# Attention with a quantising stream on VectorE: where the stream's steps and the projection jobs are placed

## The chip, the cores and the metric

One Trainium2 chip. The same program runs on all eight cores, each with one batch row of 2048 tokens. The metric is the device time of the slowest core in microseconds, the median of the runs.

## The reference

One transformer layer whose attention and feed-forward part both read the same normalised tokens:

```python
xn = _layernorm(x)                        # x: (8, 2048, 1024), one batch row a core
# attention, 16 heads of 64
q, k, v = xn @ wq.T + bq, xn @ wk.T + bk, xn @ wv.T + bv
scores = einsum(q, k) * 64 ** -0.5;  masked where x[..., 0] == 0
attn = softmax(scores) @ v;  a = attn @ wo.T + bo
# feed-forward with quantised operands, hidden size 4096
h = bit_linear(xn, w1)                    # tokens rounded to 127 steps of their largest value,
h = silu(depthwise_conv1d(h))             # weights to -1, 0, 1 by the mean of their absolute values
f = bit_linear(h, w2)
out = x + a + f
```

So the weights w1 and w2 have to be read once for the mean of their absolute values and once more to be rounded, and each token row has to be scaled and rounded, before the feed-forward part can start.

## The kernel before

Attention comes first, the feed-forward part second. This text concerns attention. Its main loop has 512 **steps**, one for each pair of a query block and a key tile: 8 head pairs times 4 query blocks of 512 are 32 iterations (`NIT`) of 16 key tiles (`NT`) each. Every engine has its program written out step by step by Python loops.

- **ACT** (`a_scalar`) takes one exponential of 128x1024 at a step (L363).
- **PE** (`a_tensor`) does at step *i*: `scores(i+1)` (L445, two matmuls into one of two halves of psS), then the **pieces** that the planner put on this step (`piece`, L386), then `pv` (L462, eight small matmuls) for the steps of `pv_at`. The values of steps 0, 1 and 2 of an iteration are put off by 2, 1 and 1 steps, to give the norm time.
- A piece is one matmul of a **job**. Jobs are: `k`, `q` and `v` (projections of head pairs or value columns, eight matmuls each, L397, L406, L413), `t` (transpose of the finished context, L419), `x` (transpose of half a quantised token tile, L425, two halves a tile) and `m` (the sum for the means of the weights, L429). Jobs take two PSUM slots in turn (`slot`): the first piece of a job waits on `pq_ev` until DVE has evicted the job two before it. An `x` piece also waits for the token tile (`xq_w`), a `t` piece for the norm (`cn_w`).
- **DVE** (`a_vector`) runs strictly in order. At step *i*: at position 1 of an iteration the `norm` of the iteration before (L594, L599: reciprocal and product, which first waits for the last values of it, and which the first values of the new iteration wait for), then the **stream** of this step (`strm_task`), then `evac` of the jobs whose last piece stood at this step (k L552, q L560 and L562, v L565 and L568, t L573, x L576).
- The stream has 64 weight chunks `w` (one sum of absolute values of 128x1024 each, L610), 16 token tiles `x` in four parts (scale L616; largest value L620; four small ones L623 to L628; round L631 and L638), `m` (L644, L645), a gap, and 64 chunks `z` in three parts (quantise a weight chunk, L652, L655, L663).
- **SP** (`a_sync`) loads the chunks and tiles of the stream into four buffers in turn; the load of item n waits until item n-4 is done.
- **POOL** (`a_gload`) loads projection weights of the next head pairs when k and q jobs are done with a buffer (L309, L311), and later the output weights.

**Two planners** in `_build` set the order. The first (L153 to L177) places the stream: five chunks to a token tile, every part at a share of the steps that goes by a table of weights, over the steps 3 to 487 other than positions 0 and 1 of an iteration. The second (L179 to L224) places the jobs: each has a due step; at each step a credit (`cap_full`, `cap_less`) says how many pieces may be taken; small jobs (t, x, m) go first; and a job may begin only some steps (`evac_steps`) after the job two before it ended. Token transposes are due two steps after the last part of their tile:

```python
for n, step in ready_x.items():
    due[("x", n, 0)] = due[("x", n, 1)] = step + 2
due[("m", 0, 0)] = ready_m + 2
```

Of the kernel before, what the change touches and what calls it, by code (L numbers as in the profile page):

```python
# [16 lines left out]
NT = T // 128  # L17
# [17 lines left out]
def _build():  # L35
# [103 lines left out]
    NW = W1CH + W2CH  # L139
    NIT = NHP * NQB  # L140
    NSTEP = NIT * NT
# [11 lines left out]

    strm_items = []
    for n in range(NT):
        strm_items += [("w", ch) for ch in range(5 * n, min(5 * n + 5, NW))]
        if 5 * n < NW <= 5 * n + 5:
            strm_items.append(("m", 0))
        strm_items.append(("x", n))
    strm_items += [("gap", 0)] + [("z", ch) for ch in range(NW)]  # L160
    weight = {"w": 2.5, "x": 4.6, "m": 1.0, "gap": 8.0, "z": 3.7}
    parts = {"w": 1, "x": 4, "m": 1, "gap": 0, "z": 3}
    total_w = sum(weight[k] for k, _ in strm_items)
    free_steps = [i for i in range(3, NSTEP - 24) if i % NT not in (0, 1)]
    step_strm = {i: [] for i in range(NSTEP)}
    ready_x, ready_m = {}, 0
    acc = 0.0
    for kind, n in strm_items:
        for part in range(parts[kind]):
            pos = acc + weight[kind] * part / parts[kind]  # L170
            i = free_steps[int(pos / total_w * len(free_steps))]
            step_strm[i].append((kind, n, part))
            if kind == "x" and part == 3:
                ready_x[n] = i
            if kind == "m" and part == 0:
                ready_m = i
        acc += weight[kind]  # L177

    step_pieces = {i: [] for i in range(NSTEP)}  # L179
    n_pieces = {"k": 8, "q": 8, "v": 8, "t": 1, "x": 1, "m": 1}  # L180
    piece_cost = {"k": 1.0, "q": 1.0, "v": 0.55, "t": 0.3, "x": 0.3, "m": 0.5}
    evac_steps = {"k": 2, "q": 3, "v": 2, "t": 2, "x": 2, "m": 2}
    cap_full = [1.2, 2.4, 2.4, 0.6, 0.6] + [1.8] * 11
    cap_less = [1.0, 2.0, 2.0, 0.4, 0.4] + [1.2] * 11
    due = {}
    for it in range(NIT):
        hp, s0 = it // NQB, it * NT
        big = [("v", (2 * it + m) % NT, 1 + (2 * it + m) // NT) for m in range(2)
               if 2 * it + m < 3 * NT]
        if hp < NHP - 1:  # L190
            big.insert(0, ("k", hp + 1, it % NQB))
        if it < NIT - 2:
            big.append(("q", it + 2, 0))
        for m, job in enumerate(big):
            due[job] = s0 + (0, 4, 8, 10)[m]
        if it >= 1:
            due[("t", it - 1, 0)] = s0 + 5
    for n, step in ready_x.items():
        due[("x", n, 0)] = due[("x", n, 1)] = step + 2
    due[("m", 0, 0)] = ready_m + 2  # L200
    wait_list = sorted(due, key=lambda jb: due[jb])
    ends = [-9, -9]
    kinds = ["v", "v"]
    cur, nxt = None, 0
    credit = 0.0
    for step in range(NSTEP):
        cap = cap_full if step < 25 * NT else cap_less
        credit = min(credit + cap[step % NT], 4.0)
        while credit > 0.3:
            if cur is None:  # L210
                ready = [jb for jb in wait_list if due[jb] <= step]
                if not ready or step < ends[-2] + evac_steps[kinds[-2]]:
                    break
                small = [jb for jb in ready if jb[0] in "txm"]
                cur, nxt = (small or ready)[0], 0
                wait_list.remove(cur)
            step_pieces[step].append((cur, nxt))
            credit -= piece_cost[cur[0]]
            nxt += 1
            if nxt == n_pieces[cur[0]]:  # L220
                ends.append(step)
                kinds.append(cur[0])
                cur = None
    assert cur is None and not wait_list, (cur, wait_list)  # L224
    first_z = min(i for i in range(NSTEP) for e in step_strm[i] if e[0] == "z")
    done_at = {jb: step for step in range(NSTEP) for jb, p in step_pieces[step]}
    assert done_at[("m", 0, 0)] < first_z and done_at[("x", NT - 1, 1)] < first_z
    assert all(done_at[("q", it, 0)] < it * NT - 2 for it in range(2, NIT))
    assert all(done_at[("k", hp, b)] < hp * 64 + 4 * b - 2 for hp in range(1, NHP) for b in range(4))
    assert all(done_at[("v", ti, q)] < q * 128 + ti - 1 for q in range(1, 4) for ti in range(NT))  # L230
    last_piece = {k: n - 1 for k, n in n_pieces.items()}
    step_jobs = {i: [j for j, p in step_pieces[i] if p == last_piece[j[0]]] for i in range(NSTEP)}
    for i in range(NSTEP):
        jobs += step_jobs[i]
# [1027 lines left out]
```

## Time and profile before

| | us |
|---|---|
| median of 3 runs (lowest, highest) | 1194.06 (1193.83, 1195.04) |
| profiled execution, its own time | 1195.17 |
| its span, slowest core (all cores 1190.2 to 1193.6) | 1193.6 |
| attention's loop, first to last exponential, in the profile | 90.4 to 650.0 |
| mean granted TensorE clock, cores | 0.984 to 0.987 |

How it is read: a row of a group gives the line, engine, tiles and shapes, the count, the busy time in us and the mean of one in ns, then the idle time of the engine before it and who ended it. A line of a timeline gives start and length in us; consecutive instructions of one line stand together with their count, and since matmuls overlap, their lengths are longer than their spacing. All rows below are of the slowest core, core 7.

### The profile page before, as it was taken

Reading aid. Unit: us, or ns where it says so; the run is one execution under the profiler, and the core shown is the slowest. Engines: PE = TensorE matmul, PEld = TensorE weight load, DVE = VectorE, ACT = ScalarE, POOL = GpSimd, SP = SyncE. Lnnn points to the kernel's source line nnn. Section 1 sums busy time; section 2 is a strip of 40 time slices with the busy share of each in tenths; the row PEclk is TensorE's granted clock in tenths of the full one; section 3 lists DMA queues with packets and bytes.
Section 4 is the critical chain, followed back from the end, with each engine's and each line's share of the span. In section 5 each row is a group of like instructions: output and inputs, shape, how many; then the busy total and the mean of one; then the engine's idle time right before and its main releaser. Section 6 shows DMA issues by size and latency. Waiting matters only on the chain.

```text
span 1193.6 us, 28386 instructions; the slowest of 8 cores (1190.2 to 1193.6 us)
## 1 busy us (share of the span) xinstructions
PE 1090.4 (91%) x9138; PEld 591.9 (50%) x9138; DVE 891.8 (75%) x1519; ACT 815.8 (68%) x1115; POOL 222.6 (19%) x177
## 2 busy tenths in 40 slices
PE   1579999999989999999988999989999999999698
PEld 0345555566555666555555444444444444444243
DVE  4646787888887888887872788877777777777676
ACT  2559888888878999999998444566666666555100
POOL 1000000000000000000022133233323333434374
PEclk9789999999999999999999999989999999999999
DMA  8636756546543676856584456564454454553252
GB/s 216 183 44 163 184 162 173 174 150 192 164 125 81 167 181 164 192 155 180 160 194 129 152 166 182 165 193 116 144 157 137 146 149 143 150 151 116 71 170 95
DMA packets 84717, 183.06 MB, mean 153 GB/s; under 512 B 25184, under 2 KB 29664, under 8 KB 84576
## 3 DMA queue, kind: packets, MB, share of 16 engines
q1 hardware_dynamic: 79248, 172.52, 49.4%
q0 software_dynamic: 4032, 8.39, 4.9%
q8 instruction: 80, 1.31, 0.5%
q14 instruction: 61, 0.50, 0.1%
q10 hardware_dynamic: 1296, 0.34, 0.1%
HBM read 164.44 MB, written 25.17 MB: 159 GB/s over the span
## 4 chain that ended last, share of the span: by engine, by line
PE 73%; ACT 12%; DVE 7%; issue 5%; DMA 1%; DVEq 0%; ACTq 0%; POOL 0%; SPq 0%; POOLq 0%
PE psC L869 17%; PE psA L887 16%; PE psS L445 13%; ACT probs L363 11%; PE psV L462 7%; PE psA L855 5%; PE psQ L397 5%; PE psQ L413 4%; PE psQ L406 3%; PE psC L887 2%; DMA xhead<-x 1%; DVE hq L1061 1%; PE psX L879 1%; PE psX L887 1%; PE psS L381 0%
## 5 line engine op out<-in xcount | busy, mean ns | idle before, releaser
L363 ACT ACTIVATE probs<-psS 128x1024 bf16<-128x1024 f32 x512 | 504.0, 1022 | 55.6 <-PE psS L445 42.3
L445 PE MATMUL psS<-qz,kroll 128*128 128x512 bf16 x1024 | 304.5, 378 | 16.7 <-ACT probs L363 12.0
L869 PE MATMUL psC<-xqT,w1q_sb 128*128 128x512 bf16 x1024 | 242.9, 381 | 0.0
L887 PE MATMUL psA<-w2q_sb,hq 128*128 128x512 fp8e4 x896 | 216.0, 382 | 16.7 <-DVE hq L1061 16.7
L462 PEld LDWEIGHTS psV<-v_sb,probs 128*128 128x128 bf16 x4096 | 183.0, 97 | 76.4 <-issue 2.1
L780 POOL TENSOR_TENSOR h_act<-h_act,shb_sb 128x512 f32<-128x512 f32 x128 | 164.3, 1286 | 251.3 <-DVE hq L1061 198.2
L462 PE MATMUL psV<-v_sb,probs 128*128 128x65 bf16 x4096 | 198.4, 193 | 0.7 <-ACT probs L363 0.5
L869 PEld LDWEIGHTS psC<-xqT,w1q_sb 128*128 128x128 fp8e4 x1024 | 99.3, 98 | 116.6 <-issue 1.9
L887 PEld LDWEIGHTS psA<-w2q_sb,hq 128*128 128x128 bf16 x896 | 87.5, 98 | 126.5 <-issue 25.2
L1010 DVE SCALAR_TENSOR_TENSOR u_sb<-psC,cws,u_sb 128x511 f32<-128x511 f32 x128 | 95.8, 749 | 71.4 <-ACT u_sb L805 71.2
L805 ACT ACTIVATE u_sb<-psC,cws 128x510 f32<-128x510 f32 (+2 forms) x128 | 87.5, 683 | 57.6 <-PE psX L879 56.1
L799 ACT ACTIVATE u_sb<-psC,edge,cws 128x1 f32<-128x1 f32 x96 | 33.8, 352 | 125.3 <-PE psC L869 125.3
L1013 DVE SCALAR_TENSOR_TENSOR u_sb<-psC,cws,u_sb 128x511 f32<-128x511 f32 x128 | 96.0, 750 | 13.7 <-DVE u_sb L1010 0.5
L1061 DVE TENSOR_SCALAR hq<-h_act,meff,meffneg 128x512 bf16<-128x512 f32 x128 | 92.5, 725 | 17.0 <-PE psX L887 9.4
L815 ACT ACTIVATE h_act<-u_sb,cbc 128x512 f32<-128x512 f32 x128 | 92.2, 720 | 0.0
L445 PEld LDWEIGHTS psS<-qz,kroll 128*128 128x128 bf16 x1024 | 67.8, 98 | 47.3 <-issue 39.4
L413 PE MATMUL psQ<-wv_sb,xnT 128*128 128x256 bf16 x512 | 77.8, 276 | 3.1 <-ACT xnT L349 1.9
L397 PE MATMUL psQ<-xnT,wqk 128*128 128x512 bf16 x256 | 78.9, 399 | 1.8 <-DVE xqT L576 1.7
L824 ACT ACTIVATE ab<-h_act 128x512 f32<-128x512 f32 x128 | 80.1, 626 | 0.1
L406 PE MATMUL psQ<-xnT,wqk 128*128 128x512 bf16 x256 | 79.1, 380 | 0.2 <-DVE xqT L576 0.2
L309 POOL DMA_DIRECT2D wqk<-wk_t x6 | 3.2, 529 | 399.9 <-PE psQ L406 399.9
L610 DVE TENSOR_REDUCE wsum<-strm 128x1 f32<-128x1024 f32 x64 | 76.9, 1211 | 0.2
(104 smaller groups left out, 1035.0 us busy)
## 6 DMA issues: line engine op xcount, KB each, us to landing
strm<-w_t SPq DMA_DIRECT2D x128, 512.0 KB, 4.3
w2q_sb<-w2q_stage SPq DMA_DIRECT2D x112, 256.0 KB, 2.6
w1q_sb<-w1q_stage SPq DMA_DIRECT2D x64, 256.0 KB, 2.9
xhead<-x SPq DMA_DIRECT2D x16, 512.0 KB, 5.6
strm<-x SPq DMA_DIRECT2D x16, 512.0 KB, 4.9
xarea<-x SPq DMA_DIRECT2D x16, 512.0 KB, 6.3
res_stage<-xarea SPq DMA_DIRECT2D x16, 512.0 KB, 3.6
xarea<-res_stage SPq DMA_DIRECT2D x16, 512.0 KB, 6.5
```

Source lines behind the costliest of these rows:

```text
L363: s.activation(out=probs[:, (i % NP) * 1024:(i % NP + 1) * 1024], in_=psS[:, (i % 2) * 1024:(i % 2 + 1) * 1024], func=AF.Exp, scale=0.125, ...
L397: mm = t.matmul(ps, wqk[:, o:o + 128], xnTv[:, p, b * 512:(b + 1) * 512], start=(p == 0), stop=(p == 7))
L406: mm = t.matmul(ps, wqk[:, o:o + 128], xnTv[:, p, qb * 512:(qb + 1) * 512], start=(p == 0), stop=(p == 7))
L413: mm = t.matmul(ps[:, 0:256], xnTv[:, p, a * 128:(a + 1) * 128], wv_sb[:, b * 2048 + p * 256:b * 2048 + (p + 1) * 256], start=(p == 0), st ...
L445: mm = t.matmul(psS[:, (g % 2) * 1024 + hh * 512:(g % 2) * 1024 + (hh + 1) * 512], kTv[:, hp % 2, kc * 128:(kc + 1) * 128], qz[:, (it % 4) ...
L462: mm = t.matmul(psV[:, hh * 512 + qt * 65:hh * 512 + (qt + 1) * 65], probs[:, o:o + 128], v_v[:, kc, 2 * hp + hh, :], start=(kc == 0 and q ...
L780: g.tensor_tensor(h_unit(r), h_unit(r), shb_unit(r), OP.mult).then_inc(sem("f_qa"), 1)
L869: mm = t.matmul(mbank(g), w1q_sb[:, o + cc * 256:o + cc * 256 + 128], xqTv[:, cc, tb * 512:tb * 512 + 512], start=(cc == 0), stop=(cc == N ...
L887: return t.matmul(gbank(k, j), hq[:, o:o + 128], w2q_sb[:, w:w + 512], start=(jc == 0), stop=(jc == NJC - 1))
L1010: v.scalar_tensor_tensor(ua[:, 1:512], ps[:, 0:511], cws[:, jc * 3:jc * 3 + 1], ua[:, 1:512], OP.mult, OP.add).then_inc(sem("f_o2"), 1)
L1013: tap3 = v.scalar_tensor_tensor(ua[:, 0:511], ps[:, 1:512], cws[:, jc * 3 + 2:jc * 3 + 3], ua[:, 0:511], OP.mult, OP.add)
L1061: v.tensor_scalar(hq_unit(r), h_unit(r), meff[:, 0:1], meffneg[:, 0:1], OP.add, OP.add).then_inc(sem("f_q"), 1)
```

## The change

The stream's plan no longer leaves positions 0 and 1 of an iteration free. The jobs are planned twice with one function, `place_jobs`. The first plan has no token and mean jobs; from it, each step gets a **room**: 1.1 us less what evictions (`evac_us`) and the norm (`norm_us`) take. The stream's parts (`part_us`) are then laid at steps so that they use the summed room in proportion. There are four chunks to a token tile in place of five, and the mean's sums stand before the last tile. Then the token jobs get due steps four (before: two) after their last part, the mean job too, and the jobs are planned again. The gap is 5.0 of the new units (before 8.0 of the old). What each engine executes is the same; the order in which it stands changes.

```diff
     for n in range(NT):
-        strm_items += [("w", ch) for ch in range(5 * n, min(5 * n + 5, NW))]
-        if 5 * n < NW <= 5 * n + 5:
-            strm_items.append(("m", 0))
-        strm_items.append(("x", n))
+        strm_items += [("w", ch) for ch in range(4 * n, 4 * n + 4)] + [("x", n)]
+    strm_items.insert(strm_items.index(("x", NT - 1)), ("m", 0))
     strm_items += [("gap", 0)] + [("z", ch) for ch in range(NW)]
-    weight = {"w": 2.5, "x": 4.6, "m": 1.0, "gap": 8.0, "z": 3.7}
-    parts = {"w": 1, "x": 4, "m": 1, "gap": 0, "z": 3}
-    total_w = sum(weight[k] for k, _ in strm_items)
-    free_steps = [i for i in range(3, NSTEP - 24) if i % NT not in (0, 1)]
...
+    part_us = {"w": [1.2], "x": [0.9, 1.2, 0.9, 1.8], "m": [0.3], "gap": [5.0],
+               "z": [0.8, 0.8, 0.9]}
+    evac_us = {"k": 0.75, "q": 1.55, "v": 0.6, "t": 0.75, "x": 0.65, "m": 1.0}
+    norm_us = 1.5
...
+    def place_jobs():
+        pieces = {i: [] for i in range(NSTEP)}
+        wait_list = sorted(due, key=lambda jb: due[jb])
+        ends, kinds = [-9, -9], ["v", "v"]
+        cur, nxt, credit = None, 0, 0
...
+        return pieces
+
+    step_pieces = place_jobs()
+    room = []
+    for i in range(NSTEP):
+        used = sum(evac_us[j[0]] for j, p in step_pieces[i] if p == last_piece[j[0]])
+        used += norm_us if i % NT == 1 and i >= NT else 0
+        room.append(1.1 - used)
+    room_at, acc = [], 0.0
+    for i in range(NSTEP):
+        acc = max(0.0, acc + room[i]) if 3 <= i < NSTEP - 24 else acc
+        room_at.append(max(acc, room_at[-1] if i else 0.0))
+    total_us = sum(sum(part_us[k]) for k, _ in strm_items)
...
+    for kind, n in strm_items:
+        for part, us in enumerate(part_us[kind]):
+            pos = acc / total_us * room_at[-1]
+            i = next(i for i in range(NSTEP) if room_at[i] > pos)
+            if kind != "gap":
+                step_strm[i].append((kind, n, part))
...
+            acc += us
     for n, step in ready_x.items():
-        due[("x", n, 0)] = due[("x", n, 1)] = step + 2
-    due[("m", 0, 0)] = ready_m + 2
...
+        due[("x", n, 0)] = due[("x", n, 1)] = step + 4
+    due[("m", 0, 0)] = ready_m + 4
+    step_pieces = place_jobs()
```

The body of `place_jobs` is the old planner's loop, unchanged.

## Rows read from the trace of the kernel before

**Rows 1.** The page, busy time of each engine over the span.
```profile
PE 1090.4 (91%) x9138; PEld 591.9 (50%) x9138; DVE 891.8 (75%) x1519; ACT 815.8 (68%) x1115; POOL 222.6 (19%) x177
```

**Rows 2.** Stretches: length, busy PE, PEld, DVE, ACT, POOL; clock, DMA share, GB/s.
```profile
619.20:650.00 30.80, 26.15 (x331) 15.68 (x327) 7.67 (x16) 30.66 (x32) 6.99 (x3) 1.00 0.67 178
...
124.50:216.80 92.30, 85.28 (x1014) 52.64 (x1013) 75.89 (x130) 79.14 (x81) 2.12 (x4) 1.00 0.61 168
216.80:234.60 17.80, 17.42 (x211) 10.79 (x209) 15.01 (x27) 15.84 (x17) 0.00 (x0) 1.00 0.46 154
234.60:342.60 108.00, 104.11 (x1223) 65.03 (x1220) 89.50 (x160) 95.19 (x97) 1.05 (x2) 1.00 0.56 168
342.60:366.10 23.50, 18.13 (x217) 10.92 (x214) 21.43 (x46) 15.63 (x17) 1.05 (x2) 1.00 0.36 91
366.10:384.00 17.90, 17.20 (x206) 11.12 (x207) 12.15 (x25) 15.99 (x17) 0.00 (x0) 1.00 0.29 71
384.00:521.70 137.70, 135.68 (x1585) 84.16 (x1584) 112.15 (x200) 126.93 (x129) 2.11 (x4) 1.00 0.72 175
486.80:521.70 34.90, 34.03 (x396) 21.14 (x394) 27.80 (x50) 31.54 (x33) 0.00 (x0) 1.00 0.75 182
```

**Rows 3.** Waits between 124.5 and 216.8 us: total, times, longest.
```profile
DVE rden L594 <- PE psV L462: 4.6, 3, 2.0
...
PE psQ L425 <- DVE kroll L552: 5.1, 5, 1.2
```

**Rows 4.** Timeline of PE around a token transpose.
```profile
205.84 0.59 PE L445 MATMUL psS<-qz,kroll 128*128 128x512 bf16 x2
206.27 0.59 PE L397 MATMUL psQ<-xnT,wqk 128*128 128x512 bf16 x2
206.70 0.41 PE L462 MATMUL psV<-v_sb,probs 128*128 128x65 bf16 x8
206.94 0.60 PE L445 MATMUL psS<-qz,kroll 128*128 128x512 bf16 x2
...
207.59 0.39 PE L419 MATMUL psQ<-identb_s,cn 128*128 128x128 bf16 x4
207.82 0.41 PE L462 MATMUL psV<-v_sb,probs 128*128 128x65 bf16 x8
...
208.86 0.59 PE L445 MATMUL psS<-qz,kroll 128*128 128x512 bf16 x2
210.54 0.38 PE L425 MATMUL psQ<-identb_s,qbuf 128*128 128x128 bf16 x4 [1.08 <-DVE kroll L552]
211.20 0.38 PE L425 MATMUL psQ<-identb_s,qbuf 128*128 128x128 bf16 x4 [0.28 <-DVE ctx L573]
```

**Rows 5.** Timeline of DVE in the same stretch.
```profile
203.45 1.22 DVE L610 TENSOR_REDUCE wsum<-strm 128x1 f32<-128x1024 f32 x1
204.59 0.81 DVE L616 TENSOR_SCALAR strm<-strm,negm,rstd 128x1024 f32<-128x1024 f32 x1
...
208.66 0.81 DVE L638 TENSOR_SCALAR qbuf<-strm,meffneg,tiny 128x1024 bf16<-128x1024 f32 x1 [0.18 <-DVE strm L631]
209.53 0.75 DVE L552 TENSOR_SCALAR kroll<-psQ,bkc 128x512 bf16<-128x512 f32 x1
210.20 0.74 DVE L573 TENSOR_SCALAR ctx<-psQ,bvc 128x512 bf16<-128x512 f32 x1
```

**Rows 6.** Waits between 342.6 and 366.1 us.
```profile
ACT probs L363 <- PE psS L445: 7.6, 6, 2.3
```

**Rows 7.** Groups of instructions over the span: evictions and the norm.
```profile
L599 DVE TENSOR_TENSOR cn<-psV,rden 128x256 bf16<-128x256 f32 x64 | 24.3, 420 | 1.2
...
L560 DVE TENSOR_SCALAR qz<-psQ,bqc 64x512 bf16<-64x512 f32 x32 | 23.7, 741 | 27.7 <-PE psQ L406 27.5
...
L576 DVE CAST xqT<-psQ 128x512 bf16<-128x512 f32 x32 | 21.4, 683 | 0.7 <-PE psQ L425 0.7
```

**Rows 8.** DMA issues of the page: count, size, us to landing.
```profile
strm<-w_t SPq DMA_DIRECT2D x128, 512.0 KB, 4.3
```

More of the change, by code:

```diff
@@ L155, in _build @@
     for n in range(NT):
-        strm_items += [("w", ch) for ch in range(5 * n, min(5 * n + 5, NW))]
-        if 5 * n < NW <= 5 * n + 5:
-            strm_items.append(("m", 0))
-        strm_items.append(("x", n))
+        strm_items += [("w", ch) for ch in range(4 * n, 4 * n + 4)] + [("x", n)]
+    strm_items.insert(strm_items.index(("x", NT - 1)), ("m", 0))
     strm_items += [("gap", 0)] + [("z", ch) for ch in range(NW)]
-    weight = {"w": 2.5, "x": 4.6, "m": 1.0, "gap": 8.0, "z": 3.7}
-    parts = {"w": 1, "x": 4, "m": 1, "gap": 0, "z": 3}
-    total_w = sum(weight[k] for k, _ in strm_items)
-    free_steps = [i for i in range(3, NSTEP - 24) if i % NT not in (0, 1)]
[L165 to L179, printed above, removed]
+    part_us = {"w": [1.2], "x": [0.9, 1.2, 0.9, 1.8], "m": [0.3], "gap": [5.0],
+               "z": [0.8, 0.8, 0.9]}
+    evac_us = {"k": 0.75, "q": 1.55, "v": 0.6, "t": 0.75, "x": 0.65, "m": 1.0}
+    norm_us = 1.5
     n_pieces = {"k": 8, "q": 8, "v": 8, "t": 1, "x": 1, "m": 1}
+    last_piece = {k: n - 1 for k, n in n_pieces.items()}
     piece_cost = {"k": 1.0, "q": 1.0, "v": 0.55, "t": 0.3, "x": 0.3, "m": 0.5}
@@ L197, in _build @@
             due[("t", it - 1, 0)] = s0 + 5
-    for n, step in ready_x.items():
-        due[("x", n, 0)] = due[("x", n, 1)] = step + 2
-    due[("m", 0, 0)] = ready_m + 2
[L201 to L223, printed above, removed]
@@ L224, in _build @@
-    assert cur is None and not wait_list, (cur, wait_list)
+    def place_jobs():
[3 more added lines that the diff above has]
+        cur, nxt, credit = None, 0, 0
+        for step in range(NSTEP):
+            cap = cap_full if step < 25 * NT else cap_less
+            credit = min(credit + cap[step % NT], 4.0)
+            while credit > 0.3:
+                if cur is None:
+                    ready = [jb for jb in wait_list if due[jb] <= step]
+                    if not ready or step < ends[-2] + evac_steps[kinds[-2]]:
+                        break
+                    small = [jb for jb in ready if jb[0] in "txm"]
+                    cur, nxt = (small or ready)[0], 0
+                    wait_list.remove(cur)
+                pieces[step].append((cur, nxt))
+                credit -= piece_cost[cur[0]]
+                nxt += 1
+                if nxt == n_pieces[cur[0]]:
+                    ends.append(step)
+                    kinds.append(cur[0])
+                    cur = None
+        assert cur is None and not wait_list, (cur, wait_list)
+        return pieces
@@ new lines, in _build @@
+    step_strm = {i: [] for i in range(NSTEP)}
+    ready_x, ready_m = {}, 0
+    acc = 0.0
+    for kind, n in strm_items:
[4 more added lines that the diff above has]
+                step_strm[i].append((kind, n, part))
+            if kind == "x" and part == 3:
+                ready_x[n] = i
+            if kind == "m":
+                ready_m = i
+            acc += us
@@ L230, in _build @@
     assert all(done_at[("v", ti, q)] < q * 128 + ti - 1 for q in range(1, 4) for ti in range(NT))
-    last_piece = {k: n - 1 for k, n in n_pieces.items()}
     step_jobs = {i: [j for j, p in step_pieces[i] if p == last_piece[j[0]]] for i in range(NSTEP)}
```

## The prediction

> **What bounds the kernel now.** I began with the busy table of the page [rows 1]: PE is the fullest engine (91%), DVE the second (75%); but that is an average over two halves, so the second view is the table of stretches. The change touches attention alone, 512 steps of one exponential each. I cut that part at the start of every 16th exponential, so a stretch holds whole query blocks of 16 steps (*blocks* 0 to 31; the ACT count is 16 for each block and one that straddles). The reader is to see four things in [rows 2]. Blocks 2 to 6 last 18.46 us each, block 7 17.8, blocks 8 to 13 18.0 each. Block 14 lasts 23.5, and there DVE is busy 21.43 us and PE only 18.13. Blocks 16 to 23, where no token tile is quantised, last 17.2 each with PE at 98%. The last two, which hold hardly any projection piece, last 15.4, so 0.96 us is the shortest step that ACT allows. PE's granted clock is 1.00 (2.4 GHz) in all these stretches, through the waits too.
>
> The third view, the waits of blocks 2 to 6, says who is late: PE waits at a token transpose for DVE's eviction of a k job, 5 times in 5 blocks, 5.1 us together [rows 3]. The timeline around one of them shows why. PE finished its scores at about 209.3 (208.86 and 0.43 for the pair, the spacing 205.84 to 206.27) and begins the first transpose at 210.54, the second at 211.20, where such a group has spacing 0.23 (207.59 to 207.82) [rows 4]. DVE ran the last part of the token's chain up to 209.47 and evicted k from 209.53 and ctx from 210.20, behind it [rows 5]; each transposed half needs the PSUM slot of the job two before it. So PE stood 1.24 + 0.43 = 1.7 us in this block. In block 14 the last three token tiles fall on 16 steps with no weight chunk left between them: the same wait comes several times, and ACT waits 7.6 us for scores [rows 6].
>
> **How I priced the change.** No instruction is added or removed: 64 chunk sums, 16 token chains, 64 chunks of quantising, the evictions and norms stay; only the step at which each stands moves. I wrote out the planner's rules of both versions into tables of what PE and DVE get at each step, and priced them. A PE step is 0.43 us of scores, 0.21 for a k or q piece (the pair from 206.27 to 206.70), half of that for a v piece of half the columns, 0.23 for a transposed half, 0.24 for values (206.70 to 206.94) [rows 4], never under 0.96 in all. DVE runs in order, an eviction after PE's last piece; a job's first piece waits for the eviction of the job two before. DVE's prices: chunk sum 1.14 from start to start (203.45 to 204.59), k or ctx 0.67 (209.53 to 210.20) [rows 5], q 1.5 for two halves of 0.74, token half 0.68, norm two multiplies of 0.42 and two short reciprocals, about 1.0 [rows 7]. One choice is left, spacings or durations: the chunk sum lasts 1.22 where the next instruction starts 1.14 after it, so neighbours overlap by 0.08 us [rows 5].
> The Trainium skill says otherwise (VectorE: DVE Perf Modes, The DRAIN you can't avoid): the next Vector instruction does not start until the pipeline of the one before has emptied. By that rule durations would be the price everywhere; the trace does not agree.
> With durations the new table is 4.9 us shorter than the old one, with spacings 6.7. Both misjudge stretches of the old kernel (durations give 25.4 us for block 14, the row 23.5), so I take the terms stretch by stretch and check them against the rows.
>
> *Block 14.* Before: three tiles. After: four chunks, one tile and the mean job, since with four chunks to a tile the sixteen tiles go evenly over steps 3 to 240, one in 15 steps. DVE's largest backlog, at 1.1 us a step, falls from 9.1 us (step 237) to 2.8 (step 33). The new tables give 17.4 and 18.1 us; I take 18.1, near the 18.0 of its neighbours: 18.1 - 23.5 = **-5.4 us**. Blocks 1 and 15: -0.3 and +0.3, nothing together.
>
> *Blocks 2 to 7.* The old wait goes: transposes are due 4 steps after the chain in place of 2, and the chain is done. What is late next is an eviction. The new plan puts a tile's two halves at steps 0 and 2 of each block, the k job right behind the second, q's last piece on step 15 and a chunk sum on step 0. From q's last piece: 0.17 until its result shows (the pair of [rows 4] lasts 0.59, its spacings 0.43), q 1.5, chunk 1.14, the first half 0.68: 3.5 us. PE comes to k after values 0.24, steps 0 and 1 at 0.96, scores 0.43 and a half 0.23: 2.8. It waits 0.7 there, each block; behind the waiting k piece stand the next scores, and ACT for them. The new plan is also lumpier: steps with no piece beside one of seven v and one of four k; an empty step costs ACT's 0.96 where PE has 0.67 of work. Both tables give +0.1 for each of blocks 2 to 6 (durations 18.45 for the old ones, the row 18.46) and +1.6 for block 7, which had no long wait before: **+2.2**.
>
> *Blocks 8 to 13.* The old plan waits in most of them (0.2 to 1.3 us by the tables); the new one in 8 and 9 (0.5 to 0.8, v behind k) and in 13 for the norm (0.6). Tables: -2.8 and -3.1; taken **-2.9**.
>
> *Blocks 16 to 23.* No long wait in either. But the job grid shifts: from block 16 on the new plan has in each block the layout that the old one reaches only in 22 and 23 (four k, three, one, none, four v ...). Those two last 17.45 each, all eight 137.7 [rows 2]: 8 x 17.45 - 137.7 = **+1.9**. Blocks 24 to 31 keep their pieces: 0.
>
> *Queues.* SP issues the same 80 loads into four buffers, each landing 4.3 us after its issue [rows 8]. The tightest run of the new plan uses four chunks in some six steps, over 5.5 us, so they stay hidden; if not, each late one costs DVE at most its landing. POOL's weight loads wait for k and q jobs that move by a few steps and are needed blocks later: nothing. The second half of the kernel is not touched.
>
> Sum: -5.4 + 2.2 - 2.9 + 1.9 = **-4.2 us**. The profiled execution took 1195.17 (span 1193.6), 1.1 over the median 1194.06; against it the sum gives 1191.0, against the median **1189.9 us**. A measurement of this kernel tells about 0.2% (2.4 us) from no change.
>
> **Rivals.**
> *The waits go altogether* (0.12). If PE never waits for a slot, blocks 2 to 13 fall to the 17.2 of those without token tiles: 218.1 - 12 x 17.2 = 11.7 less, 5.4 in block 14, 1.9 given back: 1179. For it: PE was busy 85.28 of 92.3 us in blocks 2 to 6. Against it: the arithmetic of step 2 has 0.7 us to lose.
>
> *The gain is handed back, the change does not do what it says* (0.20). DVE's room is measured on a first plan without token and mean jobs; the second plan puts 56 of the 79 evictions of the first half on another step, by up to 4. If the waits come out 0.3 us a block longer than priced in blocks 1 to 14, 4.2 is back: 1194.
>
> *DVE late at the turn of the block: slower* (0.13). The old plan keeps its stream off steps 0 and 1; the new one puts a chunk on step 0, in front of the norm of step 1, and in blocks 3, 5 and 7 one at step 15. Values of step 3 wait for the norm, k at step 2 for the eviction; by my prices the norm ends 0.6 us before it is needed. If DVE gets there 1.0 us later (a chunk ahead of q's eviction), both waits grow by it; in two thirds of 14 blocks that is +9.3: 1199. It decides from 0.3 us a block. For it: in blocks 2 to 6 DVE comes early to the norm in only 3 of 5 already [rows 3]. Against: a chunk of step 15 can run before q's last piece is there.
>
> **How the numbers follow.** The forecast case has 0.55 and its own range 1184 to 1192: with DVE 5% dearer the tables give 8 to 10 us less than before, with DVE 5% cheaper 1 to 3 (the old waits were smaller then). The larger gain has 0.12, none 0.20, slower 0.13. Range 1181 to 1197.5: it leaves out most of the largest gain and over half of the slow case, 0.18. Faster by over 0.2%: 0.12 and 0.53 of the forecast case, 0.65; within: 0.20 + 0.02 = 0.22; slower 0.13.
>
> **What would show it.** Block 14 near 18 us with DVE under 19 busy. In blocks 2 to 7 PE waits for the eviction of a token half at a k matmul, once a block, 0.7 to 1.1 long, in place of the transposes' wait for k. Blocks 16 to 23 near 139.6. The second half the same within 1 us. Wrong if block 14's time reappears in 13 or 15, if values wait for the norm in many blocks, or if the layout of blocks 16 to 23 costs nothing.

## The result, and the profile after

The changed kernel takes 1195.64 us (median of 20 runs) where the kernel before takes 1194.12: the ratio is 1.0014, with a 95% interval of 1.0007 to 1.002. It is slower by 0.14%, within the 0.2% that I called no change, though the interval leaves out 1. The forecast was 4.2 us faster. Three of the forty executions, two before and one after, were in a slower state (1308 to 1361 us); the ratio leaves them out.

In the changed kernel every line of the attention part stands 14 further down (scores L459, values L476, norm L608 and L613, chunk sum L624, eviction of a token half L590, quantising L666, L669, L677). The table of stretches of the changed kernel, cut at its own 16th exponentials: length, busy PE, PEld, DVE, ACT, POOL, clock, DMA share, GB/s.

```profile
123.60:216.90 93.30, 85.74 (x1022) 54.10 (x1021) 75.48 (x132) 79.54 (x80) 2.13 (x4) 1.00 0.57 161
216.90:236.20 19.30, 17.58 (x213) 11.16 (x212) 17.20 (x30) 15.76 (x16) 0.00 (x0) 1.00 0.55 178
236.20:342.10 105.90, 103.85 (x1235) 65.58 (x1233) 91.19 (x161) 94.85 (x97) 2.11 (x4) 1.00 0.54 166
342.10:359.70 17.60, 17.41 (x209) 11.21 (x206) 14.97 (x29) 15.87 (x17) 0.00 (x0) 1.00 0.68 180
359.70:377.30 17.60, 17.23 (x208) 10.89 (x204) 11.35 (x28) 15.83 (x18) 0.00 (x0) 1.00 0.23 55
377.30:516.90 139.60, 136.04 (x1571) 84.40 (x1569) 109.62 (x195) 126.28 (x128) 2.11 (x4) 1.00 0.66 162
...
614.60:635.30 20.70, 15.53 (x167) 9.16 (x164) 8.17 (x14) 15.51 (x16) 0.00 (x0) 0.84 0.78 202
620.00:625.00 5.00, 3.84 (x39) 2.67 (x40) 2.88 (x8) 1.02 (x1) 0.00 (x0) 0.50 1.04 267
650.70:1193.40 542.70, 517.63 (x2620) 239.20 (x2620) 411.67 (x617) 274.93 (x549) 196.95 (x141) 0.99 0.45 143
```

Set beside [rows 2]:

| blocks | before | forecast | after |
|---|---|---|---|
| 2 to 7 | 110.1 | +2.2 | 112.6 (+2.5) |
| 8 to 13 | 108.0 | -2.9 | 105.9 (-2.1) |
| 14 | 23.5 | -5.4 | 17.6 (-5.9) |
| 15 | 17.9 | +0.3 | 17.6 (-0.3) |
| 16 to 23 | 137.7 | +1.9 | 139.6 (+1.9) |
| 24 to 29 | 97.5 | 0 | 97.7 (+0.2) |
| 30 and 31 | 30.8 | 0 | 36.1 (+5.3) |

Up to block 30 the forecast nearly came true: its first exponential starts at 614.6 us where it started at 619.2. Of these 4.6 us 0.8 was there before the loop began (first exponential at 89.6 us, before 90.4), in code that the change does not touch. From there to block 30 the changed kernel takes 525.0 us where the old one takes 528.8, 3.8 less. Then block 30, one of those that keep their pieces, lasts 20.7 us where 15.4 was usual. The second half takes 542.7 us, 0.9 less than the 543.6 before; that is no more than the profiles of one kernel and another differ by in this stretch (541.7 to 544.4 over all of them). The loop as a whole lasts 561.1 us in place of 559.6, the 1.5 us by which the medians differ; the spans of these two executions (1193.4 and 1193.6) hide it. The loss is in that one block. Its chain of waits and its timelines show how (start, length, and in brackets the idle time before and who ended it). DVE:

```profile
614.63 0.76 DVE L666 TENSOR_SCALAR strm<-strm,sw 128x1024 f32<-128x1024 f32 x1 [1.41 <-DMA strm<-w_t]
...
619.64 0.75 DVE L666 TENSOR_SCALAR strm<-strm,sw 128x1024 f32<-128x1024 f32 x1 [2.08 <-DMA strm<-w_t]
620.31 0.24 DVE L608 RECIPROCAL rden<-psV 128x4 f32<-128x4 f32 x2
620.59 0.76 DVE L613 TENSOR_TENSOR cn<-psV,rden 128x256 bf16<-128x256 f32 x2
```

PE in the same stretch:

```profile
617.67 0.59 PE L459 MATMUL psS<-qz,kroll 128*128 128x512 bf16 x2 [0.41 <-ACT probs L377]
621.16 1.15 PE L476 MATMUL psV<-v_sb,probs 128*128 128x65 bf16 x16 [2.90 <-DVE cn L613]
622.12 1.04 PE L459 MATMUL psS<-qz,kroll 128*128 128x512 bf16 x2
```

The longest piece of the chain of waits there:

```profile
608.39 11.08 DMA strm<-w_t
```

The quantising part on step 480 (position 0 of block 30) waits for a chunk whose load took 11.1 us from 608.39 on, where 4.3 is the median [rows 8]. Behind it in DVE's order stands the norm of step 481; for the norm wait the values that stand on step 483 of PE, 2.90 us; behind them on PE stand the next scores, and for these ACT waits (3.88 us). PE's scores at 617.67 still have their full-clock length. After them PE stands from 618.26 on; the clock over 614.6 to 620 us is 0.95, so it falls only shortly before 620, and from 620 to 625 it is half (1.2 GHz): the two score matmuls at 622.12 last 1.04 us in place of 0.59.

What holds the load back are the output-weight loads. POOL issues eight of them, of 256 KB each, from 602.8 to 607.5 us, once the last k, q or v job (step 466) is done. The DMA engines are full (a share over 1 says that the times of the packets add up to more than the stretch of the 16 engines). The issues, and the ten microseconds before the wait ends:

```profile
L776 POOL DMA_DIRECT2D wo_bf<-wo_t x8: 527/661/1015, 602.8 to 607.5; - x8
...
610.00:620.00 10.00, 6.70 (x66) 3.30 (x65) 5.56 (x8) 9.37 (x10) 0.00 (x0) 0.97 1.07 228
```

The old kernel has the same contention, and its DVE waited for loads as well. There the same chunk belongs to step 479. DVE could start on it at 620.19, and the norm came right behind at 620.86; block 30 had begun at 619.2 and PE was not held up.

```profile
620.19 0.75 DVE L652 TENSOR_SCALAR strm<-strm,sw 128x1024 f32<-128x1024 f32 x1 [1.91 <-DMA strm<-w_t]
...
620.86 0.24 DVE L594 RECIPROCAL rden<-psV 128x4 f32<-128x4 f32 x2
```

### The profile page after: what moved, and what is told of

The parts are those of the page before. It is cut to its first block, busy times and chain, and to the rows that moved or that the text cites. A ratio compares the mean times of both kernels' runs of the same rounds, so it can differ in the third digit from the quotient of the medians.

```text
span 1193.4 us, 28386 instructions; the slowest of 8 cores (1187.5 to 1193.4 us)
## 1 busy us (share of the span) xinstructions
PE 1091.6 (91%) x9138; PEld 596.0 (50%) x9138; DVE 894.4 (75%) x1519; ACT 817.0 (68%) x1115; POOL 224.0 (19%) x177
## 4 chain that ended last, share of the span: by engine, by line
PE 74%; ACT 12%; DVE 6%; issue 5%; DMA 2%; ACTq 0%; DVEq 0%; POOL 0%; SPq 0%; POOLq 0%
PE psC L883 17%; PE psA L901 16%; PE psS L459 13%; ACT probs L377 10%; PE psV L476 7%; PE psA L869 5%; PE psQ L411 5%; PE psQ L427 4%; PE psQ L420 3%; PE psC L901 2%; DMA xhead<-x 1%; DMA strm<-w_t 1%; DVE wsum L624 1%; DVE hq L1075 1%; PE psX L893 1%
## 5 line engine op out<-in xcount | busy, mean ns | idle before, releaser
L459 PE MATMUL psS<-qz,kroll 128*128 128x512 bf16 x1024 | 305.6, 380 | 19.6 <-ACT probs L377 14.7
L476 PEld LDWEIGHTS psV<-v_sb,probs 128*128 128x128 bf16 x4096 | 184.4, 98 | 81.8 <-issue 8.7
L476 PE MATMUL psV<-v_sb,probs 128*128 128x65 bf16 x4096 | 200.4, 194 | 4.0 <-DVE cn L613 3.2
L813 ACT ACTIVATE u_sb<-psC,edge,cws 128x1 f32<-128x1 f32 x96 | 34.1, 355 | 124.5 <-PE psC L883 124.5
L1075 DVE TENSOR_SCALAR hq<-h_act,meff,meffneg 128x512 bf16<-128x512 f32 x128 | 92.4, 725 | 16.8 <-PE psX L901 9.6
L459 PEld LDWEIGHTS psS<-qz,kroll 128*128 128x128 bf16 x1024 | 68.4, 98 | 52.1 <-issue 42.0
L411 PE MATMUL psQ<-xnT,wqk 128*128 128x512 bf16 x256 | 76.5, 399 | 6.5 <-DVE xqT L590 6.5
L420 PE MATMUL psQ<-xnT,wqk 128*128 128x512 bf16 x256 | 77.9, 380 | 0.2 <-DVE xqT L590 0.2
L624 DVE TENSOR_REDUCE wsum<-strm 128x1 f32<-128x1024 f32 x64 | 76.5, 1212 | 0.2
```

What stands on the lines that cost most here:

```text
L411: mm = t.matmul(ps, wqk[:, o:o + 128], xnTv[:, p, b * 512:(b + 1) * 512], start=(p == 0), stop=(p == 7))
L420: mm = t.matmul(ps, wqk[:, o:o + 128], xnTv[:, p, qb * 512:(qb + 1) * 512], start=(p == 0), stop=(p == 7))
L459: mm = t.matmul(psS[:, (g % 2) * 1024 + hh * 512:(g % 2) * 1024 + (hh + 1) * 512], kTv[:, hp % 2, kc * 128:(kc + 1) * 128], qz[:, (it % 4) ...
L476: mm = t.matmul(psV[:, hh * 512 + qt * 65:hh * 512 + (qt + 1) * 65], probs[:, o:o + 128], v_v[:, kc, 2 * hp + hh, :], start=(kc == 0 and q ...
L1075: v.tensor_scalar(hq_unit(r), h_unit(r), meff[:, 0:1], meffneg[:, 0:1], OP.add, OP.add).then_inc(sem("f_q"), 1)
```

## The experiments

All times are medians with the ratio to the kernel before, run on the same chip.

**Output-weight loads later.** Theory A: the gain is real and one wait eats it. The edit, in the changed kernel:

```diff
         g.wait_ge(sem("pq_pe"), J_QKV)
+        g.wait_ge(sem("sm_done"), len(loads) - 3)
         for cc in range(NCH):
```

> The changed kernel, where POOL's eight loads of the output weights wait besides until all but the last three items of DVE's stream are done (they start some 8 us later). Theory A (the gain of the blocks before 30 is real, and is lost to one wait in block 30, where the quantising part at position 0 waits for an input load that lands in 11 us beside the output-weight loads, with the norm behind it): block 30 falls from 20.8 to 15.4 us, the time from 1195.6 to about 1190.4. Rival B (the end of attention is held by the stream and its stores anyway, and whoever comes early waits): within 1 us of 1195. Rival C (the clock fell for another reason, and the wait follows from it): the granted clock stays at half in 620 to 625 us and block 30 stays over 18.

Measured: 1190.63 us, ratio 0.997 (0.9958 to 0.9982). Its block 30:

```profile
614.40:629.80 15.40, 12.68 (x165) 7.93 (x164) 6.89 (x13) 15.33 (x16) 4.56 (x7) 1.00 1.02 182
```

The block is back at 15.4 and the clock at 1.00, though the DMA engines are as full as ever (1.02). POOL now issues its loads from 613.6 us on, and DVE waits for no load of the stream any more. Theory A holds. B falls. C falls as well: with the wait gone the clock does not fall, and in the changed kernel PE stood before the clock fell.

**The same on the kernel before.**

> The kernel before with the same later start of the output-weight loads. Theory A: there the norm of block 30 came at 620.9 us just in time although DVE waited twice for loads (1.9 and 2.0 us), and PE did not wait for it, so nothing changes: 1194.1 within 0.7. Rival B: if the stream holds the end of attention, freeing its loads gains here too, 1 to 3 us.

Measured: 1194.09, ratio 0.9996 (0.9986 to 1.0006). No change, as A says. The contention was there, with cover.

**The last quantising parts earlier.** The positions of the quantising parts are scaled so that the last stands at step 464:

```diff
+            if kind == "z":
+                z0 = pos if (n, part) == (0, 0) else z0
+                pos = z0 + (pos - z0) * (room_at[464] - z0) / (room_at[-1] - z0)
             i = next(i for i in range(NSTEP) if room_at[i] > pos)
```

> The changed kernel with the quantising parts squeezed so that the last stands at step 464 in place of 487, before the output-weight loads start. Nothing else of the plan moves. Theory A: no part of the stream is left in block 30, so its wait goes; 1190.4, up to 1191.5 if the denser stream costs blocks 16 to 28 a little. Rival B: since the second half's first loads wait for the last store of the stream, and that is now early, B as well allows a gain, but the second half would then be shorter as well, by over 1 us; A says that it stays the same.

Measured: 1191.36, ratio 0.9977 (0.9967 to 0.9987), at the upper end of A's figures.

```profile
615.70:631.10 15.40, 12.68 (x164) 7.94 (x164) 1.76 (x5) 15.33 (x17) 2.62 (x2) 1.00 0.82 161
```

The second half takes 544.4 us on the slowest core in that profile, no less than before, so nothing speaks for B's gain from the early stores (a difference under 1 us would not show here).

**One part moved by two steps.**

```diff
             i = next(i for i in range(NSTEP) if room_at[i] > pos)
+            if i // NT in (30,) and i % NT in (0, 1):
+                i += 2 - i % NT
```

> The changed kernel with one quantising part moved from step 480 to step 482, behind the norm of step 481; loads and their contention untouched. Theory A: the norm no longer waits for the load, so the wait of 3 to 4 us goes or falls under 1; 1190.5 to 1191.5. Rival B: PE waits at the next thing that DVE owes (the transpose of the context at step 485) for as long: within 1 us of 1195.

Measured: 1190.90, ratio 0.9968 (0.9955 to 0.9981). DVE in block 30 of that kernel (its lines two further):

```profile
616.92 0.25 DVE L610 RECIPROCAL rden<-psV 128x4 f32<-128x4 f32 x2
617.20 0.76 DVE L615 TENSOR_TENSOR cn<-psV,rden 128x256 bf16<-128x256 f32 x2
619.73 0.75 DVE L668 TENSOR_SCALAR strm<-strm,sw 128x1024 f32<-128x1024 f32 x1 [1.77 <-DMA strm<-w_t]
```

All jobs and all other parts of the stream stand on the steps of the changed kernel. The load is as late as before (619.73 against 619.64), but the norm now runs in front of it, at 616.92 in place of 620.31, and block 30 lasts 15.8 us at a clock of 1.00, so the burst by itself does not lower the clock. One instruction on the wrong side of the norm is worth the 4.7 us.

**Parts of the change.** With the loads out of the way (1190.6) I undid or varied one part at a time. First the due steps:

```diff
-        due[("x", n, 0)] = due[("x", n, 1)] = step + 4
-    due[("m", 0, 0)] = ready_m + 4
+        due[("x", n, 0)] = due[("x", n, 1)] = step + 2
+    due[("m", 0, 0)] = ready_m + 2
```

> The changed kernel with the late output-weight loads (1190.6), and the token and mean jobs due 2 steps after their last part again, as before the change. Theory A (the wait for PSUM slots is set by where token halves stand among the other jobs, not by how early they are due; with 4 steps they fall on steps 0 and 2 of blocks 2 to 7, right behind the eviction of q and a chunk sum and in front of the norm and k): with 2 steps the halves stand before the q-to-k turn, blocks 2 to 7 fall from 112.6 to about 107.5 us, blocks 8 to 13 from 105.8 to about 103, blocks 16 to 23 change their layout; 1183, and not over 1186. Rival D (the 4 steps are what removed the old wait of 1.7 us; with 2 it comes back): blocks 2 to 7 at 110 to 114, 1189 to 1194.

Measured: 1179.83, ratio 0.988 (0.9866 to 0.9895). Blocks 2 to 6, 7, 8 to 13 and 16 to 23 of it:

```profile
123.50:213.60 90.10, 86.32 (x1034) 55.18 (x1031) 77.62 (x136) 79.61 (x81) 1.84 (x4) 1.00 0.61 172
213.60:230.60 17.00, 16.80 (x199) 10.56 (x196) 15.23 (x27) 15.77 (x17) 0.00 (x0) 1.00 0.51 157
230.60:334.80 104.20, 101.08 (x1209) 63.16 (x1207) 89.34 (x159) 94.84 (x96) 1.07 (x2) 1.00 0.57 171
...
370.40:507.10 136.70, 133.98 (x1571) 83.60 (x1569) 109.26 (x195) 127.13 (x129) 2.12 (x4) 1.00 0.64 168
```

107.1 for blocks 2 to 7 (expected 107.5), 104.2 for 8 to 13 (expected 103), and blocks 16 to 23 are 2.9 us shorter. D falls: in this stream the 4 steps cost 10.8 us. The whole was 3 us better than I had expected.

Then the 4 steps in the old stream, whose planner differs:

> The kernel before with only the 4 steps in place of 2. If 4 steps are bad in themselves (they cost 10.8 us in the changed kernel: 1190.6 against 1179.8), this is slower than 1194, up to 1200. Theory A (only where the jobs come to stand counts): in this stream 4 steps put both halves of a token behind the last v job or q, away from the turn of the block: blocks 2 to 7 from 110.1 to about 106, 8 to 13 from 107.9 to about 104, block 14 stays over 23: 1187.

Measured: 1186.22, ratio 0.9928 (0.9911 to 0.9945). The same edit that costs 10.8 us in the new stream gains 8 in the old one. It has no value of its own; it shifts the grid of jobs. Blocks 2 to 7 took 106.5 us and 8 to 13 took 104.0, as expected. Block 14 stayed long, 22.4 us; on that core its clock fell as well (0.92), and PE had waited there once for 2.9 us:

```profile
334.00:356.40 22.40, 18.52 (x205) 11.23 (x206) 20.11 (x42) 15.70 (x16) 1.06 (x2) 0.92 0.41 96
```

**What makes the new wait of blocks 2 to 7.** The waits of PE there in the changed kernel, beside [rows 3] (total, times, longest), and the place of one of them:

```profile
PE psQ L411 <- DVE xqT L590: 5.2, 5, 1.1
```

```profile
142.70 0.74 DVE L574 TENSOR_SCALAR qz<-psQ,bqc 64x512 bf16<-64x512 f32 x1 [1.92 <-PE psQ L420]
...
143.46 0.76 DVE L576 TENSOR_SCALAR qz<-psQ,bqc 64x512 bf16<-64x512 f32 x1
...
144.25 1.22 DVE L624 TENSOR_REDUCE wsum<-strm 128x1 f32<-128x1024 f32 x1
...
144.95 0.39 PE L439 MATMUL psQ<-identb_s,qbuf 128*128 128x128 bf16 x4
145.50 0.69 DVE L590 CAST xqT<-psQ 128x512 bf16<-128x512 f32 x1
```

q's two halves, the chunk sum, the token half's eviction from 145.50 to 146.19, and PE's k matmul at 146.44 with 1.11 us marked behind it: the order that the prediction laid out. The experiment takes the stream off steps 0 and 1 of blocks 1 to 14 (the lines of the edit above, with `range(1, 15)` for `(30,)`):

> The changed kernel with the late output-weight loads (1190.6), and in blocks 1 to 14 the stream kept off steps 0 and 1 (its parts there go to step 2). Theory A: the chunk sum of step 0 is what makes the eviction of the first token half late, so PE's wait at k on step 2 goes from 1.8 us to under 0.8 and blocks 2 to 7 fall from 112.6 to 108; 1185. Rival E (the wait is q's eviction, 1.5 us, and the norm alone): blocks 2 to 7 stay within 1 us of 112.6, 1190.

Measured: 1180.92, ratio 0.9888 (0.9871 to 0.9904). Blocks 2 to 6:

```profile
122.90:210.40 87.50, 85.13 (x1022) 54.02 (x1020) 74.87 (x132) 79.48 (x80) 2.11 (x4) 1.00 0.61 174
```

No wait of a k matmul for a token half is left in the list of waits of that stretch, and these five blocks last 17.5 us each in place of 18.66. E falls. Up to block 12 the planner leaves every job on its step, so there the edit moves the chunk sums and nothing else. Blocks 2 to 7 gained 6.9 us where 4.6 was expected, since the wait went to nothing and not to 0.8. Another 2.3 us come from blocks 16 to 23 (137.3 us), where the jobs of four blocks changed their steps; that was not foreseen.

**Four chunks, or the room?**

> The changed kernel with the late output-weight loads (1190.6), with five chunks to a token tile again, so that the last tiles have no chunks between them. Theory F (block 14 is short because four chunks to a tile spread the tiles): block 14 goes back over 21 us, 1193 to 1196. Theory G (the room measured in us does it: a tile then gets the time that it takes, 4.8 of it, where the old weights gave a tile 4.6 against 2.5 for a chunk that takes half of that and put three tiles on 14 steps): block 14 between 17.5 and 19.5, and since the layout of the other blocks changes too (token halves at steps 4 and beyond in block 3), 1184 to 1190.

> The kernel before with four chunks to a token tile and the mean's sums before the last tile, nothing else. Theory F: block 14 falls from 23.5 to under 20 us and the time by 3 to 5 us, to 1190. Theory G: block 14 stays over 21.5, 1193 to 1196. Either way there is no part of the stream on steps 0 and 1, so no norm waits for a load in block 30.

The edits are the first hunk of the change, undone in the new kernel and done alone in the old one. With five chunks in the new kernel: 1181.42, ratio 0.9894 (0.988 to 0.9909), block 14 in 18.8 us. With four chunks alone in the old one: 1188.74, ratio 0.9957 (0.994 to 0.9973), block 14 in 18.7 us.

```profile
335.40:354.20 18.80, 17.39 (x210) 11.14 (x208) 16.83 (x40) 15.80 (x17) 0.75 (x2) 1.00 0.37 86
```

```profile
340.80:359.50 18.70, 17.23 (x205) 10.90 (x206) 15.24 (x32) 15.78 (x17) 1.05 (x2) 1.00 0.59 170
```

Both theories were half right, and I had set them up as if only one could be. Either edit alone unpacks block 14. The total of the five chunks was 2.6 us below the range that I had given for G: against the new kernel with four (1190.6) they gain 9.2 us, though four gain in the old one. Three edits, each alone, now gain 10.8, 9.2 and 9.7 us on the new kernel: 2 steps, five chunks, and the stream off steps 0 and 1. Blocks 2 to 7 fall from 112.6 us to 107.1, 105.7 and 105.7. That it is the combination that costs there, token halves on steps 0 and 2 with a chunk sum on step 0, is shown for the chunk sum alone; for the other two edits it is read from where they put the jobs. Against the kernel before on the same chip the four chunks alone gain 5.6 us (1194.37 to 1188.74), more than the whole change with its wait taken away (3.9, from 1194.49 to 1190.63).

**Does the wait of block 30 grow if PE comes earlier still?**

> The changed kernel with token and mean jobs due 2 steps after their last part, the output-weight loads as in the change. Theory H (the wait in block 30 goes with the step count: stream and output-weight loads both hang on PE's steps, so all of it starts earlier together): the wait stays 4 to 5 us, the stretch of blocks 24 to 31 lasts about 133 as in the changed kernel, and the time is 4 to 5 us over the 1179.8 of the same kernel with late output-weight loads: 1184.5. Rival I (an absolute floor: the loads land when they land, and whoever comes earlier waits for longer): blocks 24 to 31 last 140 or more, 1190 to 1195.

Measured: 1185.61, ratio 0.9924 (0.9909 to 0.9939). Block 30 of that kernel, which begins at 605.3 us, 9 us earlier:

```profile
605.30:626.20 20.90, 15.40 (x167) 9.13 (x164) 8.24 (x14) 15.55 (x17) 0.00 (x0) 0.84 0.77 203
```

20.9 us against 20.7, and blocks 24 to 31 take 133.6 us against 133.8, so H: the wait hangs on the steps and is no floor. The price of the contention is 5.8 us here (1185.6 against 1179.8) and 5.0 in the changed kernel (1195.6 against 1190.6). These medians are of different chips; by the ratios to the kernel before (0.9924 against 0.988, 1.0014 against 0.997) it is 5.3 us both times.

**The best version found.**

```diff
-        room.append(1.1 - used)
+        room.append(1.05 - used)
...
-        due[("x", n, 0)] = due[("x", n, 1)] = step + 4
-    due[("m", 0, 0)] = ready_m + 4
+        due[("x", n, 0)] = due[("x", n, 1)] = step + 3
+    due[("m", 0, 0)] = ready_m + 3
```

> The changed kernel with late output-weight loads, 3 steps and the room counted from 1.05 us a step in place of 1.1. A neighbour of the best one so far (1179.8), whose table of steps has one long wait fewer in block 15 (1.3 us): 1178.5 if the tables hold to 1 us, and within 1179 to 1181 if they can't tell such neighbours apart.

Measured: 1178.76, ratio 0.987 (0.9856 to 0.9885): 15.5 us under the kernel before by that ratio, and not to be told from the version with 2 steps (0.9866 to 0.9895). The wait in block 15 has gone as the table said, 16.8 us against 18.4 there:

```profile
352.60:369.40 16.80, 16.68 (x196) 10.58 (x195) 10.68 (x21) 15.67 (x16) 0.00 (x0) 1.00 0.14 39
```

## Why the prediction was wrong

*Block 14, blocks 2 to 7, 8 to 13, 16 to 23*: right, each within 0.8 us of its term, the layout cost of blocks 16 to 23 exact; together 3.7 us less in blocks 2 to 29 where 4.2 was forecast. The signs named for it came: block 14 at 17.6 with DVE 14.97 us busy, and five waits of a k matmul for a token half, at most 1.1 us long, 1.0 on the mean where the arithmetic had 0.7. The cause given for that wait was borne out by taking the chunk sum away.

*The step that failed is "Queues".* It took the landing of a load as 4.3 us everywhere and let the loads stay hidden. That is the median over the kernel. Beside the output-weight loads such a load took 11.1 us, and block 30, put down as 0, cost 5.3 us. The paragraph counted 80 loads, the 64 chunks for the sums and the 16 token tiles, and left out the 64 loads for the quantising, though [rows 8] counts 128 chunk loads; the late one is among those left out. It looked at POOL's loads of head weights and left out those of the output weights, which POOL issues at the end of attention; and it priced a late load as "at most its landing" for DVE, without asking who stands behind the part in DVE's order. There it was the norm, PE's values and ACT. The trace of before held the warning: DVE waited there for loads 1.91 and 1.99 us at 620 and 625 us, the first of them right in front of the norm of block 30. I had looked for DMA waits in the stretches that change their jobs and not in blocks 24 to 31, which I put down as 0 since PE's pieces there stay the same, although the stream's steps there move as well. A load waits until the chunk four before it is done; the last part of that chunk moved from step 468 to step 471. So the load that came too late was issued 9.7 us after block 29 had begun (608.39 against 598.7), in the old kernel 7.0 (610.40 against 603.4), and it took 11.1 us where the old one took at most 9.8 (610.40 to 620.19). That these 2.7 and 1.3 us are what made the wait is argued from these rows; what is shown is that moving the part behind the norm, delaying the output-weight loads, or drawing the stream's last parts forward each removes the loss.

The Trainium skill states the rule that the paragraph needed (Trainium Kernel Development and Optimization, Key Constraints): DMAs issued from SP, ACT and POOL all run on the same 16 DMA engines and interleave. The trace agrees, with 4.3 us grown to 11.1 and a share of 1.07.

*The rival "DVE late at the turn of the block"* named the right place, a part on step 0 in front of the norm, and the wrong occasion: I looked for it in blocks 2 to 15, a little in each, and it came once, in block 30, through a load. Its bound of 0.3 us a block was spent in one piece of 5.3. That 1195.6 us lies inside the stated range, near the 1194 of the rival "the gain is handed back", is luck: no case behind the range holds a late load, and the waits of blocks 2 to 13 did not come out longer by 0.3 us a block.

*Spacings or durations.* In blocks 2 to 29 the new kernel is 3.7 us shorter by the rows; the tables said 4.9 by durations and 6.7 by spacings. Both overstate the gain, the durations by less. One comparison does not settle the price.

The rule of the Trainium skill that the prediction sets against the spacings (VectorE: DVE Perf Modes, The DRAIN you can't avoid) has an exception in the same paragraph: a next op that is not held starts earlier. The overlap of 0.08 us fits this exception, so page and trace need not contradict each other there.

## What to carry to other kernels

When a plan moves work on an in-order engine, follow each moved instruction that waits for a DMA: what stands behind it, and which other queue's loads are under way at that time. A median landing time is no price for a load beside a burst. And read a scheduling change off the table of who stands in front of whom at each turn; the same edit of the due steps gained 8 us in one stream and cost 10.8 in the other, and the times expected from the tables of steps (1187 and 1183) were within about 3 us of both.

## What the hardware showed that I had not expected

The clock turned one wait into two costs. On five of the eight cores of the changed kernel it fell at the turn to block 30 or in it; on the other three it didn't. The stretch from 614.6 to 635.3 us, core 1 and core 7:

```profile
614.60:635.30 20.70, 16.76 (x209) 9.91 (x209) 6.92 (x15) 19.35 (x21) 2.77 (x2) 1.00 0.77 202
614.60:635.30 20.70, 15.53 (x167) 9.16 (x164) 8.17 (x14) 15.51 (x16) 0.00 (x0) 0.84 0.78 202
```

On core 1 PE waited 1.08 us for the norm, the clock stayed at 2.4 GHz, and block 30 lasts 16.8 us; on core 7 PE waited 2.90 us, the clock fell to 1.2 GHz, and the block lasts 20.7. It is the same with the others: where PE waited 1.1, 1.5 and 1.8 us (cores 1, 3 and 6) the clock did not fall, and the block is longer than 15.4 us by the wait and 0.3 us more; where it waited 2.2 to 3.9 us (cores 0, 2, 4, 5 and 7) the clock fell, and the block is longer by the wait and 1.8 to 2.5 us more. By this comparison, an estimate, the slow clock costs 1.5 to 2.2 us of the 4.0 to 5.9 that these cores lose in the block. Since the metric is the slowest core, a wait that is long on some cores counts in full.

The Trainium skill says that the default state of the clock is the throttled one and activity releases it (TensorE: Matmul & The Clock Gate, Part 1: The HAM clock gate). The trace agrees: the fall follows the wait, and with the wait taken away it does not come.
